# Who copies the centred chunks out of PSUM in the norm stages of a twelve-sublayer decoder: two chunks to VectorE, two on ScalarE

## What is computed

```python
def _layernorm(x, axis=-1, eps=1e-05):
    m = jnp.mean(x, axis=axis, keepdims=True)
    v = jnp.var(x, axis=axis, keepdims=True)
    return (x - m) / jnp.sqrt(v + eps)
...
    x = x + _L0_attn_ref(_layernorm(x, axis=-1), ...)
    x = x + _L0_xattn_ref(_layernorm(x, axis=-1), ctx_1024, ...)
    x = x + _L0_ffn_ref(_layernorm(x, axis=-1), ...)
...
    x = x + _L3_ffn_ref(_layernorm(x, axis=-1), ...)
```

## Time and profile before

| | |
|---|---|
| median of 3 runs | 2504.08 us (2503.83 to 2508.21) |
| span of the profiled execution, first to last instruction | 2491.9 us |
| between that span and the median | 12.2 us |

### The profile page before, as it was taken

The page is one execution under the profiler, slowest core; times in us unless marked ns, Lnnn a source line. Parts: engine busy times, 40 slices in busy tenths (PEclk is TensorE's granted clock), DMA queues, the critical chain, the costliest instruction groups (busy, mean ns, idle before and its releaser), DMA issues. The chain is left out here.

```text
span 2491.9 us, 36889 instructions
## 1 busy us (share of the span) xinstructions
PE 1871.6 (75%) x11751; PEld 1114.7 (45%) x11763; DVE 1741.7 (70%) x5569; ACT 1133.9 (46%) x3141; POOL 707.5 (28%) x617
## 2 busy tenths in 40 slices
PE   6996889863887999979997876556555565556778
PEld 2654447442455666644464554333333332333343
DVE  4235353268775666657746777999999999996655
ACT  3652442251315777731233554555555555554411
POOL 1200045005433333310032411344333333331130
PEclk8988899965998999989998887666666666667979
DMA  5000000310000000000200000000000000000000
GB/s 214 2 1 1 28 28 29 122 44 1 2 2 1 2 2 1 0 1 0 95 1 1 1 1 1 1 1 1 1 1 1 1 1 1 1 1 1 1 1 17
DMA packets 10592, 37.76 MB, mean 15 GB/s; under 512 B 1344, under 2 KB 7488, under 8 KB 9136
## 3 DMA queue, kind: packets, MB, share of 16 engines
q1 hardware_dynamic: 8880, 33.04, 3.4%
q0 software_dynamic: 1536, 2.59, 0.4%
HBM read 30.15 MB, written 5.51 MB: 14 GB/s over the span
## 5 line engine op out<-in xcount | busy, mean ns | idle before, releaser
L3724 PE MATMUL psum<-work 32*128 32x256 f32 x512 | 129.2, 648 | 291.9 <-ACT work L3842 291.9
L3904 DVE MATCH_REPLACE8 work<-work 128x256 f32<-128x256 f32 x768 | 305.4, 408 | 0.0
L3967 POOL TENSOR_TENSOR work<-work 128x1024 f32<-128x1024 f32 x63 | 148.3, 2354 | 487.0 <-ACT work L3842 487.0
L3901 DVE MAX8 work<-work 128x8 f32<-128x256 f32 x768 | 266.7, 409 | 0.0
L3724 PEld LDWEIGHTS psum<-work 32*128 32x128 f32 x512 | 76.8, 307 | 317.7 <-ACT work L3842 160.4
L709 POOL TENSOR_TENSOR work<-work 128x256 f32<-128x256 f32 (+2 forms) x144 | 133.5, 946 | 225.8 <-DVE work L997 225.8
L925 ACT ACTIVATE work<-work 128x128 f32<-128x128 f32 (+1 forms) x320 | 144.9, 454 | 19.4 <-DVE work L972 18.0
L3842 ACT ACTIVATE work<-work 128x256 f32<-128x256 f32 x256 | 128.2, 501 | 0.0
L3749 PE MATMUL psum<-work,tiles 128*8 128x256 f32 x512 | 116.7, 608 | 8.5 <-ACT work L3852 7.6
L3969 POOL TENSOR_TENSOR work<-work 128x1024 f32<-128x1024 f32 x63 | 119.3, 1894 | 6.1 <-DVE work L3926 1.2
L3840 ACT ACTIVATE work<-psum,work 128x256 f32<-128x256 f32 x256 | 117.5, 459 | 0.0
(11 more groups left out here) (620 smaller groups left out, 4644.8 us busy)
## 6 DMA issues: line engine op xcount, KB each, us to landing
big_weights<-L0f_dram SPq DMA_DIRECT2D x1, 6117.5 KB, 29.4
big_weights<-L_dram SPq DMA_DIRECT2D x1, 5772.0 KB, 17.6
big_weights<-L_dram SPq DMA_DIRECT2D x1, 4952.5 KB, 16.1
choice_rows<-tiles SPq DMA_DIRECT2D x2, 1024.0 KB, 10.3
tiles<-choice_rows SPq DMA_DIRECT2D x8, 256.0 KB, 4.9
big_weights<-L_dram SPq DMA_DIRECT2D x1, 2027.0 KB, 20.4
big_weights<-L_dram SPq DMA_DIRECT2D x1, 1630.5 KB, 13.9
big_weights<-L0f_dram SPq DMA_DIRECT2D x1, 1630.5 KB, 6.2
```

Of the source, the lines that this page charges most:

```text
L3724: mm = nc.tensor.matmul(scores(n)[:, u, :], qb[head, tile % 2, u % 2 * P:(u % 2 + 1) * P], kb[head, tile % 2, :], start=True, stop=True, t ...
L3901: ch.step(v.max(top8[:, n % 2, u, r, :], src[:, u, :]))
L3904: ins = v.match_replace(raw[:, n % 2, u, :], top8[:, n % 2, u, r, :], src[:, u, :], REPLACED)
L3967: ch.link(g.tensor_tensor(mine, mine, rest[:, n % 2], ALU.subtract))
```

## The change

For the 16 centred calls, VectorE copies chunks 0 and 1 out of PSUM, each after its square, at the head of its program in front of the first reciprocal (behind the additions of `before`). They have a signal of their own, `copied_v`. ScalarE keeps copies 2 and 3, in the diff behind the second root; the words that come with the change put them in front of it. Everybody who waited for a copy waits for the one of the new owner.

```diff
--- before.py
+++ after.py
@@ -73,7 +73,7 @@
 
     SIGNALS = [
         "loaded", "loaded_ahead", "stored", "var_ready", "centred", "squared", "normed", "rooted", "inverted", "spread",
-        "copied", "product_ready", "product_taken", "product_taken_v", "staged", "proj_ready", "scores_ready",
+        "copied", "copied_v", "product_ready", "product_taken", "product_taken_v", "staged", "proj_ready", "scores_ready",
         "scores_max", "probs_ready", "sums_inverted", "probs_picked", "probs_turned", "turned_copied", "turned_copied_s",
         "qk_ready", "qk_taken", "v_ready", "v_taken", "out_added", "mixed_ready", "mixed_taken", "out_turned",
         "out_copied", "out_product", "aux_pe", "aux_v", "aux_s", "aux_p", "aux_pe2", "aux_v2", "aux_s2", "aux_pe3",
@@ -252,6 +252,12 @@
         else:
             eng.wait_ge(c.normed.sem, c.normed.at(2 * i + 2))
 
+    def wait_copied(eng, i):
+        if i < 2:
+            eng.wait_ge(c.copied_v.sem, c.copied_v.at(i + 1))
+        else:
+            eng.wait_ge(c.copied.sem, c.copied.at(i - 1))
+
     def quarter(n, s):
         return slice(n * HF + s * Q, n * HF + (s + 1) * Q)
 
@@ -294,7 +300,7 @@
                 pe.wait_ge(c.inverted.sem, c.inverted.at(lo // 4 + 1))
                 for n in range(lo, hi):
                     if centre and 2 <= n <= 5:
-                        pe.wait_ge(c.copied.sem, c.copied.at(n - 1))
+                        wait_copied(pe, n - 2)
                     if n == 7:
                         pe.wait_ge(c.normed.sem, c.normed.at(1))
                     if n == 6 and also is not None:
@@ -353,7 +359,7 @@
 
             def scale(n):
                 if centre:
-                    dve.wait_ge(c.copied.sem, c.copied.at(n // 2 + 1))
+                    wait_copied(dve, n // 2)
                 if times is not None:
                     dve.wait_ge(c.weighted.sem, c.weighted.at(n // 2 + 1))
                 dve.wait_ge(c.spread.sem, c.spread.at(n + 1))
@@ -376,6 +382,9 @@
                                                before[3][:, ch[i]], ALU.add, ALU.add).then_inc(c.product_taken_v.sem, 1)
             for i in range(0 if times is None else NC):
                 nc.vector.tensor_tensor(dst[:, ch[i]], src[:, ch[i]], times[:, ch[i]], ALU.mult).then_inc(c.weighted.sem, 1)
+            for i in range(2 if centre else 0):
+                dve.wait_ge(c.squared.sem, c.squared.at(i + 1))
+                nc.vector.tensor_copy(kept_in[:, ch[i]], c.psum[:, i, :]).then_inc(c.copied_v.sem, 1)
             invert(0)
             scale(0)
             scale(1)
@@ -443,10 +452,9 @@
             square(2)
             root(0)
             square(3)
-            keep(0)
             root(1)
-            for i in range(1, NC):
-                keep(i)
+            keep(2)
+            keep(3)
             if also is not None:
                 for pair in range(2):
                     nc.scalar.activation(std2[:, pair, :], c.psum[:, stats[pair], 0:Q], ACT.Sqrt, bias=c.w(also[1])) \
@@ -494,7 +502,8 @@
         c.added_by_vector.advance(2)
     if centre:
         c.centred.advance(NC)
-        c.copied.advance(NC)
+        c.copied.advance(2)
+        c.copied_v.advance(2)
     twice = 1 if also is None else 2
     if also is not None:
         c.normed_also.advance(2 * NC)
```

## The result

The changed kernel takes 2486.31 us in the median (2481.41 to 2487.08, 4 runs) against 2503.95 us for the kernel before: a ratio of 0.992, 95% interval 0.990 to 0.994.

A forecast was written before the change was run, and what follows sets the result against it. No engine is full: a chain of stages bounds the kernel, with the last copy holding spreads 5 to 7. Terms 0.4+0.6+0.3+3.1+0.8 = 5.2 us off 2504.1 gave 2498.9 us, range 2495.0 to 2503.2.

The forecast's parts named there:

- Copy 0 free: ScalarE's copy of chunk 0 was hidden in a 0.75 us wait before the second root, so removing it gives nothing.
- copy 3 holding spreads 5 to 7 by 0.47 us: In a norm stage, ScalarE's last copy delays TensorE's spreads 5 to 7 by 0.47 us, with no idle time booked.
- The plain stage's 0.12 us: Stages that end with their last scale gain 0.12 us; three plain stages at full clock give 0.4 us.
- The two norms with additions: Two stages with a gain and an addition shared by GpSimd and VectorE gain 0.4 us each, 0.8 together.
- The direct sum, 5.2: Savings over all centred stages, 0.4+0.6+0.3+3.1+0.8 = 5.2 us, for a time of 2498.9 us.
- the term of the eight stages with projections or router: TensorE's streams behind eight norms end earlier: four by 0.45 us, four starting at lower clock by 0.33, 3.1 us in all.
- the 12.2 us around the span: Difference between median 2504.1 us and profiled span 2491.9 us, taken to lie around the span and stay unchanged.
- the first (2502.2): Rival: only the last scales count, TensorE's lead being given back; 16 x 0.12 = 1.9 us, 2502.2; chance 0.22.
- the second: Rival: the whole hold on the spreads comes off in every centred stage; 7.5 us, 2496.6; chance 0.18.
- The third: Rival: VectorE's copies and ScalarE's squares take turns at PSUM, stretching squares 1 and 2; slower, 2518; chance 0.05.
- The fourth: Rival: VectorE's load counts, 32 x 0.69 = 22 us more on its path; slower, 2526; chance 0.02.
- The fifth: Rival: copies 2 and 3 before ScalarE's second root, as worded, not behind it; same time, no case of its own.

The follow-up runs named there:

- e3: Against the kernel before, VectorE copies chunk 1 only; ScalarE keeps copy 0 before the second root, copies 2 and 3 behind it: ratio 0.9902.
- e4: Against the kernel before, VectorE copies chunk 0 only; ScalarE copies chunks 1, 2 and 3 behind the second root: ratio 1.0004.
- e6: The changed kernel plus one unread ScalarE copy behind the second root, ahead of copy 2, in 16 centred stages: ratio 0.9996 to the kernel before.
- e1: The kernel before, unchanged, measured and traced once more: ratio 0.9997, median 2507.8 us.
- e2: The changed kernel, unchanged, measured and traced once more: ratio 0.9913 to the kernel before, median 2485.5 us.
- e8: The changed kernel plus one unread 128x256 matmul on TensorE behind spread 3: ratio 0.9884 to the kernel before, median 2477.0 us.
- e7: The kernel before, no copy moved, plus one unread 128x256 matmul on TensorE between spreads 2 and 3 of 15 centred stages: ratio 0.9942.
- e5: The changed kernel with ScalarE's copies 2 and 3 put in front of the second root: ratio 0.9914 to the kernel before.

## Why the prediction was wrong

**Right, by its steps.** Copy 0 free: e3 and e4 show it. Copy 1's removal as the cause, copy 3 holding spreads 5 to 7 by 0.47 us where the list of waits shows nothing: e6 puts 0.46 us back and loses all. VectorE's copies at 0.69 us and no cost, with 0.59 us to spare (0.5 said). The plain stage's 0.12 us: 0.13. The projections' first pass 0.45 us sooner: it starts 1.18 us behind the second reciprocal in e1 and 0.73 in e2 (lines below), and these stages end 0.45 us sooner in e8 than in e7. The two norms with additions: 0.48 each, 0.4 said. The direct sum, 5.2: between 4.6 and 6.2. The two routers gave 0.76 and 0.70 in it, but part of that is the clock's, for e7 spends 0.77 and 0.59 us at 1.2 GHz in them and e8 none.

**Wrong: the term of the eight stages with projections or router.** The prediction said that starting 0.45 us earlier ends 0.45 us earlier, and took off a little where "part of the lead is used at half rate". It saw the lower clock in the 24 passes at 178 us, 0.51 us a pass on average, and treated it as given: it priced the lead at whatever clock the trace had. But here the clock depends on when TensorE's work comes, and the change alters that: e7 moves no copy and adds one matmul, and the falls are gone; e6 delays copies by 0.46 us, and they are back. Three of the four stages that were to give 0.33 us each gave 2.1 to 2.2, the fourth 3.45. The missing term is 3 x 1.7 + 3.0 = 8.1 us in those four stages alone (e1 less e7), of the 12.4 us by which the forecast fell short. The rest lies in stages whose clock differs from trace to trace, and outside the norm stages; it wasn't taken apart. The bound "the whole hold comes off everywhere", 7.5 us, was no bound for the same reason, and so the range ended too high, at 2495.0.

What TensorE did around the fall can be read from windows of the stage near 177 us: the 1.56 us from the second reciprocal's end to the fall in e1, the same length in e2, and the 2 us behind. In e1, where the clock falls at 178.59:

```profile
177.03:178.59 1.56, 1.56 (x20) 1.32 (x19) 1.35 (x4) 1.54 (x2) 0.87 (x2) 1.00 0.00 0
178.59:180.59 2.00, 2.00 (x3) 0.67 (x2) 2.00 (x5) 0.81 (x2) 0.57 (x1) 0.50 0.00 0
...
178.21 2.59 PE L329 MATMUL psum<-tiles,big_weights 128*128 128x512 f32 x3
```

and in e2, where it stays (L335 is the projection):

```profile
175.85:177.41 1.56, 1.51 (x18) 1.05 (x19) 1.29 (x5) 1.27 (x1) 1.04 (x2) 1.00 0.00 0
177.41:179.41 2.00, 2.00 (x6) 0.91 (x5) 1.93 (x5) 1.38 (x2) 0.39 (x1) 1.00 0.01 4
...
176.58 2.84 PE L335 MATMUL psum<-tiles,big_weights 128*128 128x512 f32 x6
```

In e1 the projections begin 0.38 us ahead of the fall; in e2 they begin 0.83 us ahead of the same moment, and in the 2 us behind it TensorE works on six passes, in e1 on three. TensorE isn't busier in e2 before that moment (1.51 us, for 1.56), and its idle gap ahead of the last spreads is the longer one (0.85 us before spread 4, in e1 0.36 before spread 3). The Trainium skill (TensorE: Matmul & The Clock Gate, What's actually happening) says that the clock gate follows how busy TensorE has recently been. e7 agrees in kind, one matmul more taking the falls away; the busy times of these two stretches don't show it. Why the earlier start keeps the clock up is open; that it does in these four stages is what e6 and the traces without the hold show.

**Wrong too: the 12.2 us around the span.** The prediction added them to one trace and took them as fixed. e1 shows 2 us; the other 10 come of setting one short execution beside the median of other runs. This moved no term of the sum.

The rivals: the first (2502.2) fell, for the streams keep their lead to the end (0.45 us from e7 to e8); the second pointed the right way by luck, for its 7.5 us left the clock out. The third fell in the trace: squares take 0.60 us beside VectorE's copies, as before. The fourth, VectorE's load, fell too: 22 us of copies on the busier engine came at no cost that shows. The fifth, the words' order, gave the same time, as said.

## What to carry to other kernels

Look past the list of waits: where an engine is busy with the one piece it may run while three others are held back, no idle time is booked, and only narrow windows that count instructions show it. And where a stream of matmuls begins behind sparse work, price an earlier start at both clocks: compare the granted clock at the stream's head, and try one matmul that nobody reads in the wait ahead of it, which here gave 0.6% of the kernel with nothing else changed. Before any of this, take a second trace of the same kernel.

## What was not expected of the hardware

The falls of the clock repeat in part. Near 177, 248, 500 and 2290 us each came in all four traces with the hold and without the extra matmul (the first, e1, e4 and e6) and in none of those without the hold (the first of the changed kernel, e2, e3 and e5), so these four belong to the program and not to chance. Others differ between executions of the same kernel: the stages at 1357 and 2330 us had no fall in the first trace and one in e1. VectorE's MAX8 on 128x256 read 409 ns on average in the first trace and 475 ns in e1, for the same instructions, while the stretch that they fill took 767.6 us in both: there a mean duration of one operation says nothing of the time that the stretch takes.
